# Zero-padding half-row products to 128 rows, completing the shared-key maxima one key tile sooner, and moving the down-weight products behind the last group's second key tile

## What is computed

```
def _L0_attn_ref(x, Wqd, Wqu, Wqr, Wkvd, Wku, Wvu, Wkr, Wo):    # 16 heads of 16, latent 64, rotary 64
    ql = x @ Wqd
    q = (ql @ Wqu).reshape(...)                   # "nope" part of the queries
    qr = _apply_rope((ql @ Wqr).reshape(...), cos, sin)
    ckv = x @ Wkvd
    k = (ckv @ Wku).reshape(...)                  # "nope" part of the keys
    v = (ckv @ Wvu).reshape(...)
    kr = _apply_rope((x @ Wkr)[:, None], cos, sin)[:, 0]
    scores = (q . k + qr . kr) * scale            # causal, softmax, times v, @ Wo

def _L0_ffn_ref(x, W_gate, W_qkv):                # 16 query heads that share one key and one value,
    ...                                           # selected per token by the best of 16 gates
    y = softmax(q . k_shared) @ v_shared          # causal

def _L1_ffn_ref(...):                             # Hadamard-transformed gated feed-forward;
    ...                                           # its down weights pass through a 1024-point transform
```

## Time and profile before

| | |
|---|---|
| median of 3 runs | 1003.43 us (1002.65 to 1004.03) |
| the profiled execution | 1004.49 us, its span 1002.4 us |
| mean granted TensorE clock | 0.905 of 2.4 GHz |
| busy: PE, DVE, ACT, POOL | 878.3, 556.0, 386.8, 224.8 us |

### The profile page before, as it was taken

The page is one execution under the profiler, slowest core; times in us unless marked ns, Lnnn a source line. Parts: engine busy times, 40 slices in busy tenths (PEclk is TensorE's granted clock), DMA queues, the critical chain, the costliest instruction groups (busy, mean ns, idle before and its releaser), DMA issues.

```text
span 1002.4 us, 11937 instructions
## 1 busy us (share of the span) xinstructions
PE 878.3 (88%) x4799; PEld 507.1 (51%) x4799; DVE 556.0 (55%) x988; ACT 386.8 (39%) x476; POOL 224.8 (22%) x207
## 2 busy tenths in 40 slices
PE   3898979999899899979579998888999889978997
PEld 2353534354334434424348886533333258778776
DVE  4673566775567467611443354595777426944452
ACT  2502424444343445435451331304555764500340
POOL 2571001323012302342210100500111146610010
PEclk9975999999699979979788998956999989979899
DMA  6594414532921390020400002658000061000001
GB/s 172 126 174 194 63 32 75 117 68 78 160 33 43 92 204 28 1 72 1 147 0 1 1 1 87 137 116 129 2 2 1 2 219 44 1 1 1 1 1 43
DMA packets 35647, 66.81 MB, mean 67 GB/s; under 512 B 5908, under 2 KB 14652, under 8 KB 35524
## 3 DMA queue, kind: packets, MB, share of 16 engines
q1 hardware_dynamic: 35016, 65.92, 28.5%
q10 hardware_dynamic: 576, 0.13, 0.1%
HBM read 45.93 MB, written 16.29 MB: 62 GB/s over the span
## 4 chain that ended last, share of the span: by engine, by line
PE 65%; DVE 20%; ACT 6%; DMA 5%; POOL 2%; issue 2%; SPq 1%; ACTq 0%; DVEq 0%; POOLq 0%
PE psD L1595 11%; PE psA L1595 11%; PE psO L1716 10%; DVE mx L1199 9%; PE psD L1661 9%; PE psA L1679 8%; PE psO L1595 7%; PE psA L1678 3%; DVE hid_low L1509 2%; PE psD L1663 2%; DMA Kr<-d_kn 1%; ACT Pr L907 1%; PE psA L1627 1%; ACT Pr L912 1%; SPq L483 1%
## 5 line engine op out<-in xcount | busy, mean ns | idle before, releaser
L1199 DVE TENSOR_REDUCE mx<-psD 128x1 f32<-128x512 f32 (+3 forms) x416 | 259.3, 658 | 129.4 <-PE psD L1663 93.3
L907 ACT ACTIVATE Pr<-psA 128x1024 f32<-128x1024 f32 (+3 forms) x192 | 161.8, 866 | 202.3 <-PE psA L1679 193.1
L776 POOL TENSOR_SCALAR_AFFINE_SELECT Pr<-Pr 128x512 f32<-128x512 f32 x96 | 61.2, 637 | 442.0 <-ACT Pr L907 356.0
L912 ACT ACTIVATE Pr<-psA 128x1024 f32<-128x1024 f32 (+3 forms) x96 | 63.5, 702 | 65.5 <-PE psA L1679 65.0
L1716 PE MATMUL psO<-Pr,Vh 128*32 128x512 f32 (+3 forms) x768 | 82.3, 509 | 3.7 <-POOL Pr L776 3.1
L1678 PE MATMUL psA<-Qr,Kr 128*128 128x512 f32 (+3 forms) x192 | 78.7, 423 | 2.8 <-DMA Qr<-mrow 2.8
L1663 PE MATMUL psD<-maskq,identb 128*128 128x128 bf16 x348 | 73.5, 236 | 0.0
L1679 PE MATMUL psA<-Qr,Kr 113*128 113x512 f32 (+3 forms) x192 | 66.7, 355 | 0.0
L1661 PE MATMUL psD<-Kg,Qs 96*128 96x512 bf16 (+3 forms) x192 | 56.6, 335 | 8.7 <-DVE mx L1199 6.9
L1661 PE MATMUL psD<-Kr,Qr 80*128 80x512 bf16 (+3 forms) x166 | 59.3, 390 | 4.2 <-DVE mx L1199 3.2
L1661 PE MATMUL psD<-Ks,Qs 96*128 96x512 bf16 (+3 forms) x166 | 56.3, 371 | 3.9 <-DVE mx L1199 3.2
(11 more groups left out here) (402 smaller groups left out, 1693.6 us busy)
## 6 DMA issues: line engine op xcount, KB each, us to landing
Qr<-d_qr SPq DMA_DIRECT2D x18, 512.0 KB, 11.9
d_qr<-WB SPq DMA_DIRECT2D x9, 512.0 KB, 2.6
Pr<-d_cb SPq DMA_DIRECT2D x8, 512.0 KB, 7.6
Qs<-d_gq SPq DMA_DIRECT2D x24, 128.0 KB, 4.8
Qs<-d_q SPq DMA_DIRECT2D x24, 128.0 KB
Ks<-d_k SPq DMA_DIRECT2D x24, 128.0 KB
Qr<-d_qn SPq DMA_DIRECT2D x18, 128.0 KB, 8.0
Kr<-d_kn SPq DMA_DIRECT2D x18, 128.0 KB, 8.9
```

Of the source, the lines that this page charges most:

```text
L776: pool.affine_select(out=block_, in_=block_, pattern=[[0, GH], [1, P]], compare_op=ALU.is_ge, fill=0.0, base=0, channel_multiplier=-1).the ...
L907: act.activation(place[:, h, q0:T], src[:, q0:T], ACT.Exp, scale=score_scale(i)).then_inc(a_drained, 1)
L912: act.activation(place[:, h:h + 2, q0:T], src[:, :, q0 - HALF:HALF], ACT.Exp, scale=score_scale(i)).then_inc(a_drained, 1)
L1199: dve.tensor_reduce(mx[:, j, part, h0:h0 + nh], src, AX, ALU.max).then_inc(d_drained, 1)
```

## The change

It has three parts.

1. `wq_low` is computed and multiplied on 128 rows. Nope and value products use all 128 rows of `lat`; the weights get a zero half for it (`w_ku` moves to a place of its own), written by three memsets of DVE at the start.
2. `max_end(g)` replaces MAX_END: 4 for shared-key groups beyond group 1 (3, 5, 7), else 5. Their maxima stand beside one key tile less, and their row is made one key tile sooner.
3. The four Hadamard products and DVE's scaling move from the start of group 7 into its key tile 1.

```diff
-MAX_END = 5
+def max_end(g):
+    return 4 if is_shared(g) and g > 1 else 5
...
+    if (i, kt) == (2 * NG - 1, 1):
+        return [("wdn", u) for u in range(FC // 2)]
...
-        return [(0, kt) for kt in range(KEY_KT, MAX_END)]
-    tail = [(i - 2, kt) for kt in range(MAX_END, NT) if i - 2 >= first and not is_mla(i)]
-    return tail + [(i - 1, kt) for kt in range(MAX_END)]
+        return [(0, kt) for kt in range(KEY_KT, max_end(1))]
+    tail = [(i - 2, kt) for kt in range(max_end(i - 1), NT) if i - 2 >= first and not is_mla(i)]
+    return tail + [(i - 1, kt) for kt in range(max_end(i))]
...
+        w_ku = WA[:, 6400:6400 + D]
...
-            load(w_u[LAT:P, :], ins["Wku"], w0_in)
+            load(w_ku[LAT:P, :], ins["Wku"], w0_in)
...
-                        if kt == MAX_END and i + 1 in groups:
+                        if i + 1 in groups and kt == max_end(i + 1):
                             maxima_row(i + 1)
...
-                    if i == 2 * NG - 1:
-                        down_weights()
                     for kt in range(NT):
-                        if nxt is not None and kt == MAX_END:
+                        if nxt is not None and kt == max_end(nxt):
                             maxima_row(nxt)
+                        if (i, kt) == (2 * NG - 1, 1):
+                            for u in range(FC // 2):
+                                down_weights(u)
...
+            for w in (w_u[LAT:P, :], w_ku[0:LAT, :], w_vu[0:LAT, :]):
+                op = dve.memset(w, 0.0)
+            op.then_inc(zeros_ready, 1)
...
-            dve.tensor_tensor(wq_low[0:LAT, :], WA[0:LAT, 2 * DC * P:2 * DC * P + 2 * T], wq_high[0:LAT, :],
+            dve.tensor_tensor(wq_low[:], WA[:, 2 * DC * P:2 * DC * P + 2 * T], wq_high[:],
                               ALU.subtract).then_inc(q_parts_ready, 1)
...
-                    if i == 2 * NG - 1:
-
-                        pe.wait_ge(butterflies, 1)
-                        for u in range(FC // 2):
-                            pe.matmul(d_unit(), had[:], fT8[:, 2 * u:2 * u + 2, :].rearrange("p c d -> p (c d)"),
-                                      start=True, stop=True).then_inc(d_filled, 1)
...
-                                   (wq_low[0:LAT, tile_cols(m)], lat_parts[0:LAT, c])]).then_inc(d_filled, 1)
+                                   (wq_low[:, tile_cols(m)], lat_parts[:, c])]).then_inc(d_filled, 1)
...
-            ql = lambda k, c: lat[0:LAT, c]
-            kvl = lambda k, c: lat[LAT:P, c]
+            latents = lambda k, c: lat[:, c]
...
-                    if u < 2:
-                        features(lambda k: w_u[0:LAT, tile_cols(u)], ql, [0])
-                    else:
-                        features(lambda k: w_u[LAT:P, tile_cols(u - 2)], kvl, [0])
+                    features(lambda k: (w_u, w_ku)[u // 2][:, tile_cols(u % 2)], latents, [0])
                 elif item[0] == "v0":
-                    value_units(kvl, lambda k: w_vu[LAT:P, :], [0])
+                    value_units(latents, lambda k: w_vu, [0])
```

More of the change, by code:

```diff
@@ L382, in d_attention @@
                 nxt = i + 1 if i + 1 in groups else None
-                if i == 2 * NG - 1:
-                    names.append(("wdn", FC // 2))
                 for kt in range(NT):
-                    if nxt is not None and kt == MAX_END:
+                    if nxt is not None and kt == max_end(nxt):
                         names.append((f"mrow{nxt}", 1))
@@ L448, in build @@
         dve_step, pool_step = sem("dve_step"), sem("pool_step")
-        v_cleared, rotated = sem("v_cleared"), sem("rotated")
+        v_cleared, rotated, zeros_ready = sem("v_cleared"), sem("rotated"), sem("zeros_ready")
         ln_var, ln_std, xn_ready = sem("ln_var"), sem("ln_std"), sem("xn_ready")
@@ L1236, in outputs, with down_weights @@
                         stats((4 * b, 4 * b + 4))
-            def down_weights():
-                dve.wait_ge(w1_in, 16 * N_W1)
-                for u in range(FC // 2):
[L1242 to L1247, removed]
+            def down_weights(u):
+                if u == 0:
+                    dve.wait_ge(w1_in, 16 * N_W1)
+                src = take().rearrange("p (j d) -> p j d", j=2)
+                for k in range(2):
+                    m = 2 * u + k
+                    op = dve.scalar_tensor_tensor(w_dn[:, m, :], src[:, k, :], su[:, DC + m:DC + m + 1], ws_dp,
+                                                  ALU.mult, ALU.mult)
+                op.then_inc(d_drained, 1)
             def magnitudes():
@@ L1789, in some_maxima @@
                                     continue
+                                if unit[0] == "wdn":
+                                    down_weights_unit(unit[1])
+                                    continue
                                 if unit == MAX_UNITS[0]:
@@ L1841, in rope_unit, with down_weights_unit @@
                 product(d_unit(), [(wq_high[:, tile_cols(m)], lat_parts[:, c]),
-                                   (wq_low[0:LAT, tile_cols(m)], lat_parts[0:LAT, c])]).then_inc(d_filled, 1)
+                                   (wq_low[:, tile_cols(m)], lat_parts[:, c])]).then_inc(d_filled, 1)
+            def down_weights_unit(u):
+                if u == 0:
+                    pe.wait_ge(butterflies, 1)
+                pe.matmul(d_unit(), had[:], fT8[:, 2 * u:2 * u + 2, :].rearrange("p c d -> p (c d)"),
+                          start=True, stop=True).then_inc(d_filled, 1)
             def selected_unit(j):
```

1 line of the change is left out of this document (added).

## The result

The changed kernel takes 997.18 us, median of 12 runs (993.36 to 1003.12), beside 1003.67 for the kernel before on the same chip (12 runs): ratio 0.9943 by all runs (0.9935 by the two medians), 95% interval 0.992 to 0.9966. The prediction said 997.4. On another chip it measured 996.37 (8 runs), ratio 0.9928 (0.9899 to 0.9957). The profiled execution took 1000.94 us with a span of 999.2.

The account below looks back on a forecast made before the run. It took PE, 65% of the chain, as the bound, with stretches at half clock and waits. Terms -6.7 + 2.2 - 1.5 = -6.0 us on the 1003.43 median gave 997.4, own range 992 to 1001, 8-in-10 range 991 to 1002.5.

Parts of the forecast that it names:

- Part 1, value products and nope: Ahead of group 0: padding to 128 rows lets PE's clock rise, so group 0 starts 6.7 us sooner; ends 0 and 9.
- The 1.6 us for nope 0 and 2: Ahead of group 0: padded, these products no longer overlap, adding 1.6 us to PE, hidden by its next wait.
- the wait that the prediction named: PE's 4.95 us wait for the key rows ahead of group 0, said to cover the 1.6 us.
- Part 1, rotation: Rotation's `wq_low` product: lasts as long on 128 rows as on 64, so its padding was priced at nothing.
- Part 2: Starts of groups 3 and 5: wait passes from row to later key rows, 1.1 us lost at each, +2.2 us.
- The argument that the later key rows keep this time from being won back: Groups 4 and 6: key rows hang on work behind tile 3, now after 37 units instead of 32, so land later.
- Rival 2: Groups 4 and 6: DVE paces the earlier tiles, key rows come 3.3 us later each, slower at 1008.4; chance 0.08.
- Part 3: Group 7: PE's wait for the butterflies gives way to one for POOL's mask; -1.5 us, ends -4 and +1.
- Sum: Whole kernel: -6.7 + 2.2 - 1.5 = -6.0 us, applied to the median of 1003.43, giving 997.4.
- Rival 3: Groups 3 and 5: the row was the true limit, key rows come in time, PE keeps its clock; 986, chance 0.08.
- -15 over two starts: Groups 3 and 5: part 2's remote end, key rows no later and clock kept, from 6.2 and nearly 3 each.

Follow-up runs that it names:

- values_64: Changed kernel with only the value products back on 64 rows, nope 1 and 3 still on 128: 1002.98 us, ratio 0.9987 to the kernel before.
- low_query_64: Changed kernel with only the `wq_low` product of each rotation unit back on 64 rows: 1005.54 us, ratio 1.0017 to the kernel before.
- row_at_5: Changed kernel without its second part, the row of maxima completing at tile 5 for every group: 996.19 us, ratio 0.9907 to the kernel before.
- rotation_sooner: Changed kernel with the second rotation of groups 2 and 4 at key tile 1 instead of 2: 982.46 us, ratio 0.978 to the kernel before.

## Why the prediction was right, and where only its sum was

**Part 1, value products and nope: right.** Forecast -6.7 at G0, measured -7.1 in the profiles, or -6.0 counted from the products ahead of the change. Over all traces, 96.90 to 100.17 with 64-row value products, 90.25 to 93.50 with padded ones: means 98.1 and 92.1, 6 us. The saving inside the value products was smaller (7.19 to 6.25), that behind them larger. The value products carry the larger part: with them on 64 rows and nope 1 and 3 padded, G0 still came 26.81 us behind their start, between the 22.2 to 23.8 of the padded kernels and the 28.2 to 29.9 of the others. That the number of rows matters and not only how busy PE is, which the prediction inferred from one stretch, values_64 shows as a cause: it changes nothing else. The 1.6 us for nope 0 and 2 was priced rightly and was hidden, but by DVE's pace in the rotations and not by the wait that the prediction named. The Trainium skill (TensorE: Matmul & The Clock Gate, Part 1) has the clock follow how busy PE has been; the trace disagrees, at 7.19 us of dense 64-row products without a rise.

**Part 1, rotation: wrong, the step that failed.** "The rotation's `wq_low` product lasts as long on 128 rows as on 64 ...: nothing." The duration was the wrong column. Products of a unit start 0.23 us apart where both have 128 rows, as the rows at 31.63 and 31.86 show, and 0.43 apart where 64 rows and 128 take turns. The front of low_query_64, at the same clock:

```profile
31.67 0.50 PE L1604 MATMUL psO<-lat_parts,wq_high 128*128 128x512 f32 x1
32.10 0.49 PE L1604 MATMUL psO<-lat_parts,wq_low 64*128 64x512 f32 x1
```

And the same edit stands in groups 2 and 4, in eight units each. There it is worth 1.7 to 2.0 us at each group at equal clock. By A and C as they came it is 4.9 to 6.6 us together, with the clock down for longer in the 64-row traces, and by the medians 4.6 (1000.77 to 996.19) with the row at 5 and 8.4 (1005.54 to 997.18) with it at 4. I had looked at the front alone, where it shortens the rotation and only lengthens the wait behind it, from 4.95 to 8.41.

**Part 2: the mechanism right, the price too low.** The wait did pass to the key rows, 4.27 and 4.25 us where I had 5, and the clock behind it was 0.50. "At 0.60 us for two that is 5 x 0.30 = 1.5 us on PE" was right for PE alone, 1.4 us in group 6. What the prediction put at nothing is that PE also waits longer for DVE: tiles 0 to 3 grew by 2.2 us in group 6 and, at equal clock, by 2.2 to 2.6 in groups 2 and 4. Part of it is PE's stop for DVE's output scaling, once in group 2 and once in group 4. These two lines are from the waits of PE, before and changed:

```profile
PE psD L1595 <- DVE otmp L1229: 1.5, 2, 0.8
```

```profile
PE psD L1604 <- DVE otmp L1234: 4.0, 2, 2.0
```

The argument that the later key rows keep this time from being won back holds: B and D give back 0.8 and 0.5 of it, F, which has no such rows to wait for, 1.9. At equal clock the trace has some 3.4 us net, as it came 4.8. By three pairs of medians it is +1.0 (997.18 beside 996.19), +4.8 (with `wq_low` on 64 rows) and +6.0 (with the rotation sooner). I had +2.2. Rival 2's mechanism, DVE's pace, was there in part, less than its 3.3 us a group: without the padded `wq_low` the change would have missed its gain (1005.54), and without any padding it is slower (1009.61).

**Part 3: right in its order of events, its size not told.** Forecast -1.5, shown 0.4 to 1.9 in F, with the medians 3.7 apart in intervals that overlap. The wait for POOL's mask ended at 432.6. The same mask ends at 437.5 in the kernel before (436.85 plus 0.64), 4.9 later, near the lead that group 6 had at its key tile 4, 4.3 us.

**Sum.** The lead of 6.6 us at key tile 4 of group 7 is -7.1 at G0, -4.3 in A to F from the kernel before to row_at_5, most of it `wq_low`'s (2 x 1.7 at equal clock), and +4.8 from there by the row, 1.4 of it the clock in C. I had -6.7, -1.5 for the second and +2.2 for the third. So two misses of nearly 3 us cancel, and that the median came within 0.3 us of 997.4 is luck.

**Rival 3.** The row as the true limit fell: with the key rows in time the row at tile 5 is faster than at tile 4, by 6 us in the medians (the ends of the two intervals still overlap) and by 3.0 at key tile 4 of group 7 in the traces. But what the prediction held for remote, key rows in time and a clock that stays up, is what one line brings. It priced that at -15 over two starts, though its own terms, 6.2 and 3 at each, give 18; rotation_sooner won 18.8 in B and D.

## What to carry to other kernels

A wait named for a small copy that shares its moment with a large burst of loads may be the burst's. Before moving the small thing, look at what was issued beside it and ask what holds the burst back. Here the rotation's store did, and moving that by one tile won 18 us. Price a product by the distance between starts, not by its duration, and price every place where the edited function is used. And before two stretches of two traces are compared, compare how long the clock was down in each.

## What the runs showed of the chip

- Dense products on 64 rows left PE at 1.2 GHz for 7.19 us in four traces of four; with zero rows added to them it reached 2.4 GHz before they ended, in ten traces of ten. Once up, 64-row products ran at 2.4 GHz too (1.98 us for four).
- The same short stop of PE is followed by a fall of the clock in some executions and not in others. In values_64 PE stops for the same 1.98 us as in the changed kernel at the same instruction, and the clock stays at 1.00 behind it:

```profile
223.26 0.50 PE L1604 MATMUL psD<-lat_parts,wq_high 128*128 128x512 f32 x1 [1.98 <-DVE otmp L1234]
```

```profile
224.00:228.00 4.00, 4.00 (x24) 1.92 (x23) 3.36 (x6) 0.96 (x2) 0.00 (x0) 1.00 0.08 32
```

- In row_at_5 PE stops for 1.17 and 0.45 us within the second rotation of group 2 and of group 4 alike; from 216 to 224 the windows show 0.78 and 0.80, from 308 to 320 1.00 throughout. The kernel before shows 1.00 in group 2 and 0.60 and 0.55 from 320 to 328 in group 4. What decides it stays open. In A and C the low stretch lasted 6.8 or 10.2 us in the five places where it came with 64-row rotation products, 3.4 us in eleven of thirteen with 128-row ones and 6.8 in two, both with the rotation sooner.
